# Preparation of one-core weights: a share of the down butterflies moved to GpSimd, in-place scaling on ScalarE, new orders

## The reference, cut to what matters

```
x = fwht(xn * SU_ug) / SCALE                      # over 512
x = silu(x @ W_gate.T * ws_gate) * (x @ W_up.T * ws_up)   # 2048 wide; ws_* are Wscale_ug * SCALE
x = fwht(x * SU_dp) / SCALE                       # over 2048
out = x @ W_down.T * (Wscale_dp * SCALE)
```

## Time and profile before

| | us |
|---|---|
| median of 3 runs | 2009.38 |
| lowest, highest | 2008.37, 2010.47 |
| the profiled execution | 2009.64 |
| its span in the profile | 2007.9 |
| busy PE / DVE / ACT / POOL | 1892.9 / 1461.1 / 1013.1 / 140.7 |
| first matrix product of the loop | 206.6 |

### The profile page before, as it was taken

One profiled execution on the slowest core, in us unless ns is written; L12 is line 12 of the kernel. 1 busy time (PEld: TensorE's weight loads), 2 busy tenths in 40 slices (PEclk: granted clock), 3 DMA queues, 4 the chain that ended last, 5 costly groups with the idle time before them and its releaser, 6 DMA issues.

```text
span 2007.9 us, 39473 instructions
## 1 busy us (share of the span) xinstructions
PE 1892.9 (94%) x13490; PEld 1346.5 (67%) x13490; DVE 1461.1 (73%) x3291; ACT 1013.1 (50%) x2243; POOL 140.7 (7%) x142
## 2 busy tenths in 40 slices
PE   5556899999999999999999999999999999999999
PEld 2234777767686776767686767767686767767675
DVE  6896586867677686867677686868677686868676
ACT  6845554536363544546363544545363545445363
POOL 0000010101000010101000010101000000101010
PEclk9768899999999999999999999999999999999999
DMA  7310112121212112121212121131212111131212
GB/s 258 121 47 11 40 44 52 38 54 54 54 43 52 45 42 49 38 54 54 54 49 47 44 46 47 38 59 50 54 54 44 53 40 43 40 67 38 55 54 53
DMA packets 147963, 109.36 MB, mean 54 GB/s; under 512 B 110030, under 2 KB 111158, under 8 KB 147254
## 3 DMA queue, kind: packets, MB, share of 16 engines
q1 hardware_dynamic: 147238, 105.51, 19.5%
q10 hardware_dynamic: 528, 1.05, 0.2%
HBM read 72.18 MB, written 8.65 MB: 40 GB/s over the span
## 4 chain that ended last, share of the span: by engine, by line
PE 90%; DVE 2%; issue 1%; DVEq 1%; ACT 0%; DMA 0%; SPq 0%; ACTq 0%
PE bank L824 87%; PE bank L891 1%; PE bank L645 1%; PE bank L636 1%; DVE wug L540 0%; DVE wi L580 0%; DVEq L525 0%; DVE wd L425 0%; DVE big L425 0%; PE bank L868 0%; PE bank L869 0%; DMA cvx<-in_L_attn_u_dram 0%; DMA xnT<-cvx 0%; SPq L750 0%; DVE wo L426 0%
## 5 line engine op out<-in xcount | busy, mean ns | idle before, releaser
L824 PE MATMUL bank<-xnT,wug 128*128 128x256 f16 x6144 | 708.1, 273 | 17.3 <-issue 17.3
L824 PEld LDWEIGHTS bank<-xnT,wug 128*128 128x128 f16 x6144 | 601.1, 98 | 119.8 <-issue 19.9
L824 PE MATMUL bank<-wd,h 128*128 128x512 f16 x1536 | 371.0, 379 | 0.0
L824 PEld LDWEIGHTS bank<-wd,h 128*128 128x128 f16 x1536 | 148.3, 100 | 157.2 <-issue 3.4
L824 PE MATMUL bank<-wi,xnT 128*128 128x512 f16 (+1 forms) x1152 | 204.3, 330 | 19.0 <-DMA xnT<-cvx 18.0
L983 ACT ACTIVATE tg<-bank,gate_scale 128x256 f32<-128x256 f32 x256 | 119.9, 468 | 174.8 <-PE bank L824 139.4
L1076 POOL TENSOR_TENSOR vw<-v,dec 128x512 f32<-128x512 f32 x64 | 73.9, 1154 | 1828.1 <-ACT v L1026 1374.3
L1032 ACT ACTIVATE Mx<-Mx,cs_own 128x128 f32<-128x128 f32 x512 | 162.1, 389 | 49.2 <-DMA Mx<-cs_rows 49.2
L1160 DVE SCALAR_TENSOR_TENSOR cvx<-xc,conv,cvx 128x256 f32<-128x256 f32 x384 | 169.1, 481 | 14.5
L824 PEld LDWEIGHTS bank<-wi,xnT 128*128 128x128 f16 x1152 | 100.7, 99 | 109.6 <-issue 25.3
L824 PE MATMUL bank<-xnT,wi 128*128 128x256 f16 x1536 | 172.9, 273 | 0.0
(11 more groups left out here) (237 smaller groups left out, 2308.1 us busy)
## 6 DMA issues: line engine op xcount, KB each, us to landing
Mx<-cs_rows SPq DMA_DIRECT2D x128, 256.0 KB, 3.4
cvx<-in_L_attn_u_dram SPq DMA_DIRECT2D x17, 512.0 KB, 3.4
Mx<-in_L_attn_u_dram SPq DMA_DIRECT2D x16, 512.0 KB, 3.8
out_dram<-Mx SPq DMA_DIRECT2D x16, 512.0 KB, 2.8
big<-in_L_ffn_W_down_dram SPq DMA_DIRECT2D x2, 2048.0 KB, 11.8
wug<-in_L_attn_in_proj_w_dram SPq DMA_DIRECT2D x2, 2048.0 KB, 15.8
pair<-in_L_ffn_W_gate_dram SPq DMA_DIRECT2D x4, 1024.0 KB, 5.4
pair<-in_L_ffn_W_up_dram SPq DMA_DIRECT2D x3, 1024.0 KB, 9.0
```

Of the source, the lines that this page charges most:

```text
L824: ins = nc.tensor.matmul(out, lhsT, rhs, start=first and n == 0, stop=last and n == len(pairs) - 1)
```

## The change

Four things. ACT scales the down weights' four row blocks in place as soon as they are loaded (`dsc0` to `dsc3`); the squares `dsq` then read scaled rows and take a constant factor. POOL does all four butterfly stages of the second half of the down rows, eight operations of 128x2048, when all four scalings are done; DVE keeps the first half (`db00`, `db10`, `db20`, `db30`). The down units are turned by plain transposes, and `dg` with its diagonal matrices is gone. The four lists are planned anew: nat1 is loaded ahead of dn0, `in` comes behind nat2, dn2 behind nat3; `pk` comes earlier in all lists, `db30` after it, and DVE's wo7 comes before H43.

```diff
--- before.py
+++ after.py
@@ -76,26 +76,26 @@
 PREP_PE = """
-T0 fs0 T1 nb0 H0 fs1 T2 H1 H2 T3 T4 T5 T6 H3 H4 fs2 nb1 H5 T7 T8 H6 nb2 H7 fs3 nb3 T9 T10 H8 nb4 T11 T12 nb5
-H9 H10 fs4 T13 H11 T14 H12 T15 H13 T16 fs5 H14 T17 H15 T18 H16 T19 fs6 T20 H17 H18 T21 H19 H20 T22 fs7 T23 H21
-H22 T24 T25 T26 H23 H24 T27 H25 T28 H26 T29 H27 H28 T30 T31 H29 T32 H30 T33 pk T34 H31 T35 H32 H33 T36 H34 H35
-T37 H36 T38 T39 H37 H38 T40 H39 T41 T42 H40 T43 H41 H42 T44 H43 T45 H44 H45 T46 T47 H46 H47
+fs0 T0 T1 T2 H0 T3 H1 fs1 T4 T5 H2 H3 H4 T6 nb0 fs2 H5 T7 H6 nb1 T8 T9 H7 T10 T11 fs3 nb2 H8 fs4 nb3 H9 nb4
+T12 H10 H11 nb5 T13 T14 T15 fs5 H12 H13 T16 H14 fs6 T17 H15 T18 H16 H17 T19 T20 fs7 T21 H18 H19 T22 H20 H21
+T23 H22 H23 T24 H24 T25 T26 T27 H25 H26 T28 H27 pk T29 T30 T31 H28 H29 H30 T32 T33 H31 H32 T34 H33 T35 T36 H34
+H35 T37 H36 T38 T39 H37 T40 H38 H39 T41 T42 H40 H41 T43 H42 T44 H43 T45 T46 H44 T47 H45 H46 H47
 """.split()
 PREP_ACT = """
-sq0 nq0 T0 sq1 T1 H0 T2 T3 T4 H1 H2 T5 nq1 H3 sq2 nq2 H4 T6 H5 nq3 sq3 T7 H6 nq4 T8 H7 T9 T10 nq5 H8 dsq0 H9
-H10 T11 T12 sq4 T13 H11 T14 T15 wi0 H12 sq5 dsq1 dsq2 dsq3 H13 wi1 H14 sq6 T16 wi2 T17 T18 wi3 H15 H16 T19 sq7
-H17 T20 H18 T21 H19 T22 H20 H21 T23 T24 T25 T26 H22 H23 H24 T27 T28 H25 T29 T30 H26 H27 H28 H29 T31 T32 T33
-T34 H30 H31 T35 pk H32 H33 wo0 wo1 H34 T36 wo2 T37 H35 wo3 T38 H36 T39 H37 wo4 T40 H38 wo5 T41 H39 H40 T42 wo6
-T43 H41 H42 T44 T45 H43 H44 wo7 T46 H45 T47 H46 H47
+sq0 nq0 T0 T1 sq1 T2 H0 T3 dsc0 dsq0 H1 T4 sq2 H2 dsc1 T5 T6 H3 H4 H5 T7 nq1 sq3 T8 T9 nq2 nq3 H6 sq4 nq4 H7
+T10 T11 nq5 H8 H9 H10 sq5 T12 T13 dsc2 H11 dsq1 H12 dsq2 dsc3 dsq3 wi0 T14 H13 H14 T15 T16 wi1 sq6 wi2 H15 T17
+wi3 T18 T19 sq7 H16 H17 T20 H18 T21 H19 H20 T22 H21 H22 T23 H23 T24 H24 T25 T26 H25 T27 T28 T29 H26 pk wo0 wo1
+H27 wo2 T30 H28 wo3 wo4 T31 H29 T32 H30 T33 H31 T34 H32 H33 T35 wo5 T36 H34 T37 H35 T38 H36 H37 T39 H38 T40
+wo6 T41 H39 H40 T42 T43 H41 wo7 T44 H42 T45 H43 T46 H44 T47 H45 H46 H47
 """.split()
 PREP_DVE = """
-ba0 bb0 nb0 ba1 fs0 bb1 db00 H0 H1 fs1 ba2 H2 bb2 H3 fs2 H4 H5 nb1 ba3 bb3 H6 nb2 fs3 nb3 ba4 nb4 bb4 H7 H8 H9
-nb5 ws fs4 ba5 H10 bb5 H11 wi0 H12 db01 db10 fs5 ba6 H13 H14 wi1 fs6 H15 wi2 wi3 dg bb6 H16 ba7 db11 H17 H18
-H19 H20 fs7 db20 bb7 H21 H22 db21 db30 H23 H24 H25 db31 H26 H27 H28 H29 pk H30 H31 wo0 H32 H33 H34 wo1 H35 wo2
-H36 H37 wo3 H38 H39 H40 H41 H42 wo4 H43 H44 wo5 wo6 H45 H46 wo7 H47
+ba0 bb0 ba1 fs0 bb1 fs1 H0 ba2 bb2 H1 nb0 H2 fs2 db00 H3 H4 ba3 H5 bb3 fs3 nb1 ba4 nb2 H6 bb4 nb3 fs4 H7 nb4
+H8 ba5 H9 nb5 ws bb5 ba6 H10 H11 H12 db10 wi0 fs5 wi1 H13 fs6 wi2 H14 H15 wi3 db20 H16 H17 H18 H19 bb6 ba7 bb7
+H20 H21 H22 fs7 H23 pk H24 H25 H26 db30 H27 H28 H29 H30 wo0 H31 H32 H33 wo1 H34 H35 wo2 H36 wo3 H37 wo4 wo5
+wo6 H38 H39 H40 H41 H42 wo7 H43 H44 H45 H46 H47
 """.split()
 PREP_SP = """
-wo1 dn0 nat1 in nat2 nat3 nat4 nat5 dn2 nat6 nat7 wo2
+wo1 nat1 dn0 nat2 in nat3 dn2 nat4 nat5 nat6 nat7 wo2
 """.split()
...
-        wi_scales, wi_high, wi_split, down_squared, diag_made, down_mixed = (sem(n) for n in ("wi_scales", "wi_high", "wi_split", "down_squared", "diag_made", "down_mixed"))
+        wi_scales, wi_high, wi_split, down_squared, down_scaled, down_mixed, pool_mixed = (sem(n) for n in ("wi_scales", "wi_high", "wi_split", "down_squared", "down_scaled", "down_mixed", "pool_mixed"))
...
-            down_diag = [bc_nat[:, :, :].rearrange("p a n -> p (a n)")[:, t * P:(t + 1) * P] for t in range(4)]
...
@@ -319,6 +318,17 @@
                 pool.wait_ge(consts_made, 4)
+                pool.wait_ge(down_scaled, 4)
+                for st in range(4):
+                    a, b = down_stage(st)
+                    vs = a[:, half_rows(1), :].rearrange("p t (m c w) -> p (t m) c w", c=2, w=P << st)
+                    vd = b[:, half_rows(1), :].rearrange("p t (m c w) -> p (t m) c w", c=2, w=P << st)
+                    if st == 1:
+                        pool.wait_ge(down_squared, KD)
+                    if st:
+                        pool.wait_ge(pool_mixed, 2 * st)
+                    pool.tensor_tensor(vd[:, :, 0, :], vs[:, :, 0, :], vs[:, :, 1, :], ALU.add).then_inc(pool_mixed, 1)
+                    pool.tensor_tensor(vd[:, :, 1, :], vs[:, :, 0, :], vs[:, :, 1, :], ALU.subtract).then_inc(pool_mixed, 1)
                 pool.sem_inc(prepared, 1)
@@ -374,12 +384,14 @@
+                    elif k == "dsc":
+                        act.wait_ge(down_loaded[n // 2], 16)
+                        nc.scalar.activation(down_nat[:, n, :], down_nat[:, n, :], ACT.Copy, scale=down_scale[:, n:n + 1]).then_inc(down_scaled, 1)
                     elif k == "dsq":
                         act.drain()
-                        act.wait_ge(down_loaded[n // 2], 16)
 
                         nc.scalar.activation(wi_flat[:, (KD - 1) * 2 * DPROJ:(KD - 1) * 2 * DPROJ + FF].bitcast(BF16), down_nat[:, n, :], ACT.Square,
-                                             scale=cols[:, WS_DP + n:WS_DP + n + 1], accum_out=nsq[:, 32 + n:33 + n]).then_inc(down_squared, 1)
+                                             scale=float(FF) ** 0.5, accum_out=nsq[:, 32 + n:33 + n]).then_inc(down_squared, 1)
@@ -516,15 +528,10 @@
                         butterfly(half, mixed[n % 2], 2 * P).then_inc(mixed_done, 1)
-                    elif k == "dg":
-
-                        for t in range(4):
-                            ins = nc.vector.tensor_scalar(down_diag[t], ident[:, :], down_scale[:, t:t + 1], None, ALU.mult)
-                        ins.then_inc(diag_made, 1)
                     elif k == "db":
                         dve.drain()
                         if n < 10:
-                            dve.wait_ge(down_loaded[n], 16)
+                            dve.wait_ge(down_scaled, 2 * n + 2)
                         if n == 10:
                             dve.wait_ge(down_squared, KD)
                         a, b = down_stage(n // 10)
@@ -623,17 +630,13 @@
                         else:
                             a = n - UG_UNITS
-                            pe.wait_ge(down_mixed, 8)
-                            pe.wait_ge(diag_made, 1)
+                            pe.wait_ge(down_mixed, 4)
+                            pe.wait_ge(pool_mixed, 8)
                             src = down_nat
                         if n >= 2:
                             pe.wait_ge(wt_copied, n - 1)
                         for t in range(4):
-                            o, block_t = banks[n % 2][:, t * P:(t + 1) * P], src[:, t, a * P:(a + 1) * P]
-                            if n < UG_UNITS:
-                                ins = nc.tensor.transpose(o, block_t, ident[:, :])
-                            else:
-                                ins = nc.tensor.matmul(o, block_t, down_diag[t], start=True, stop=True)
+                            ins = nc.tensor.transpose(banks[n % 2][:, t * P:(t + 1) * P], src[:, t, a * P:(a + 1) * P], ident[:, :])
                         ins.then_inc(wt_filled, 1)
```

## The result

The changed kernel takes 1985.51 us (median of 4 runs, 1983.99 to 1986.62), the kernel before 2009.93 (2008.37 to 2010.84, also 4 runs): ratio 0.9879, interval 0.9862 to 0.9896. That is 24 us faster, where the forecast was no change (2009.5) and the range ended at 1988. The ratios under Experiments are to runs of the kernel before that were made beside each kernel; their medians were 2006.9 to 2007.7 us.

What follows compares the result with a forecast made beforehand. PE's matrix multiplies fill 94% of the span; in the preparation DVE was taken to bound from dsq3 to pk. From 2009.6 us, -5.3 + 3.2 + 2 + 2.6 - 2.6 = -0.1 gave 2009.5 us, range 1988 to 2020.

Steps and rivals of the forecast that it cites:

- The step that failed: Block loop from 206.6 us: taken as untouched by the diff and left at 1801.3 us, difference 0.
- Stage 1: Preparation until dsq3 ends: 4.1 us more ACT work, 9.5 us of idle time recovered, from 88.1 to 83 us, -5.3.
- the discount: Until dsq3 ends: only half of ACT's 20 us idle time counted as recovered, though the walked lists showed hardly any left.
- Rival (c): Four ACT scalings before dsq3 delay everything: dsq3 ends later than 87, total 2018.7 us; chance 0.25.
- Stage 2: From dsq3 to pk: DVE's own work 38.7 us plus 27 us waiting for POOL, 65.7 instead of 62.5, +3.2.
- the hold: Between dsq3 and pk: POOL's operations hold SBUF for whole instructions, so DVE stands still, taken as 27 us.
- the line: POOL's price for 2048 columns, drawn through two smaller trace rows: 3.4 us; proportion to the larger row, 4.16, was taken.
- the walk in turns: Between dsq3 and pk: DVE and POOL stepped through alternately, giving a DVE wait of 29.7 us.
- PE's turn of the peaks: Around pk: T and H units ahead on PE make its peaks work 0 to 4.5 us late, +2.
- Stage 3: From pk to H47 stored: T32 starts 16.7 us after pk, sum 42.4 instead of 39.8 us, +2.6.
- What the cheaper T wins: From pk to H47: plain turning saves PE 16 x 0.44 = 7.0 us, eaten by the late start of T32.
- Start of the loop: From H47 to the loop: wo7 stands earlier on DVE, so the input block is loaded by then, -2.6.

Runs made afterwards that it cites:

- before_spread120: The kernel before with 120 semaphore increments that nobody waits for, laid where PE waits in the preparation: 1987.21 us, ratio 0.9897.
- after_pad128: The changed kernel with 128 semaphore increments that nobody waits for in front of PE's preparation: 2017.83 us, ratio 1.0058 to the kernel before.
- dve_all_old_loads: The changed kernel with DVE doing all down butterflies and the loads in the order of the kernel before: 1977.23 us, one run.
- dve_all_products: The changed kernel with DVE doing all down butterflies and down units turned by two-pass products with the identity: 1998.71 us, one run.

## Why the prediction was wrong

**The step that failed** is the first: "That is the loop; the diff touches none of it", and with it "the loop, from 206.6 us, takes 1801.3 us and I leave it alone". The diff doesn't touch the loop's instructions, but it moves them: 128 PE instructions fewer ahead of it. No rival had this. The sign was on the page that I read, 145 packets on the instruction queue and 17.3 us of "issue" before L824 in part 5, which I passed over as part of the loop's fixed cost. In its place the runs show 23.1 us that lay in the loop: the code was fetched anew in each block because of where it began. The change removed this cost by chance: before_spread120 removes it with no other edit, after_pad128 puts it back.

Of the forecast for the preparation, which is all that the sum dealt with (the windows stand under the result):

- *Stage 1, -5.3, measured -9.7.* Direction right, size off by 4.4. The scalings are 1.99 us long, as put down. ACT's busy time grew by 2.6 (59.3 to 61.9; 4.1 put down), and its idle time fell by 12.4 (19.8 to 7.4), where half of 20 was taken. My walk through the lists had given 76 to 81, and 78.4 came; the discount, argued with "The old order was planned in the same way", was wrong. The loads alone account for 5.2 (dve_all_old_loads, one run). Rival (c) is refuted by the same row: dsq3 ended at 78.4, not beyond 87.
- *Stage 2, dsq3 to pk, +3.2, measured +7.3.* The mechanism, read from three pairs of rows of 1 us in the loop, holds for operations of 4.5 us, and the 38.7 us of DVE's own work were right (69.8 less 31.3 is 38.5). The term that was mis-sized is the hold: 31.3 us and not 27. The price of an operation was 4.50 and not 4.16, 2.7 us for eight; the proportion to the larger row was nearer than the line (3.4). Here the Trainium skill's page "GPSIMD Engine Reference", section "Elementwise — side-by-side cycle accounting", had it to 0.01 us. And the walk in turns (29.7, by the longer operations 32.4) was nearer than the discount to 27 for operations in POOL's shadow: DVE and POOL do alternate. That removing POOL's part gave 27.5, so near the 27 of the sum, is in part chance: 4.3 us of waits for ACT and PE, which the sum didn't have, came back with it.
- *PE's turn of the peaks, +2, measured +2.3.* DVE waits 2.59 us for it where it waited 0.28 before, in this row of the changed kernel, timeline of DVE:

```profile
153.29 0.28 DVE L461 TENSOR_REDUCE peak<-bank 3x1 f32<-3x128 f32 x1 [2.59 <-PE bank L652]
```

- *Stage 3, pk to H47, with that turn +4.6, measured +3.4.* T32 came 19.2 us after pk (16.7 + 2 put down), and 24.0 us later H47 was stored (25.7 put down). "What the cheaper T wins, 16 x 0.44 = 7.0, is eaten by the late start of T32": dve_all_products has the 7.2, the row of pk and T32 the rest.
- *Start of the loop, -2.6, measured -1.3.* The load was issued at 186.8 and there before H47 was stored, but 1.34 us of "issue" came in its place before the statistics, in this row of DVE's timeline:

```profile
192.63 1.29 DVE L1108 BATCH_NORM_STATS2 stats<-cvx 128x6 f32<-128x512 f32 x2 [1.34 <-issue]
```

The trace names what fills it: the thirteen semaphore increments with which DVE's code of the loop begins (L1088), one each 0.09 us, from 191.41 to 192.54. In the kernel before they stood from 190.6 to 191.7, hidden in the wait for the load. The view of that line in the changed kernel:

```profile
L1088 DVEq EVENT_SEMAPHORE  x13: 21/21/21, 191.4 to 192.5; - x13
```

The four errors (-4.4, +4.1, -1.2, +1.3) nearly cancel, so that the sum for the preparation was right by luck, though the mechanism of its decisive term, the hold, was not. The whole was wrong by the loop alone.

## What to carry to other kernels

In a kernel with a long loop, look at the instruction queue in part 3 of the page and at "issue" before the loop's products: packets that grow with the number of iterations say that the loop's code is fetched each time, and any edit that changes the number of that engine's instructions ahead of the loop can switch that on or off. Before crediting an edit with a gain, see in which stage it lies, and shift the code alone as a control; here every comparison of two preparations had to be read by the loop's start, not by the total. Giving elementwise work with two SBUF inputs to POOL while DVE has such work too cost more here than it saved: an operation that takes DVE 2.2 us held it for some 4, and the kernel was 14 us slower than with all of it on DVE. And a difference between two runs prices a term net of the waits that it covered: to price the term itself, compare the steps.

## What the runs showed of the hardware

- PE's loop of 1704 instructions is loaded once where it starts 14 or 22 instructions behind a multiple of 256 (counted from the program's own first instruction), and nine packets of 16 KB are loaded in each of 16 blocks where it starts 62, 82, 102 or 150 behind. The loss is 0.2 to 0.3 us a block at the first three and 1.2 to 1.5 at 150. The Trainium skill, page "Runtime: NRT & Kernel Launch", section "Instruction fetch mechanics", says that PE holds 2048 instructions in a FIFO filled in blocks of 256; packet size and the fact that 1704 instructions can stay agree. Its sentence that a taken branch out of a window of two pages forces a fetch doesn't fit this loop, which goes back over at least seven pieces and at 14 and 22 fetches nothing after its first block. By 2048 alone all of these places would fit, so something takes more than the loop. Some 50 instructions in front and one piece kept for loading ahead would do (the estimate above); no run tested it.
- DVE and POOL alternate operation by operation when both want SBUF. A DVE operation of 0.23 us (128x16) took 4.46 beside POOL's of 4.5, one with a single SBUF tensor, a scalar column and a constant (128x4) 3.50 instead of 0.23, those on 128x1 nothing more.
- A semaphore increment that nobody waits for takes PE 0.15 to 0.16 us (120 of them in front, from 0.7 us on, put the first product at 19.4) and DVE 0.09 (thirteen in 1.2 us).
